# One queue for the first loads, queries ahead of the modulation's rows, and spare products in TensorE's pauses

## The reference, cut to what matters

```python
mod = (silu(L0_c) @ L0_wmod).reshape(4, 6, 1, -1)
sa, ca, ga, sb, cb, gb = (mod[:, i] for i in range(6))     # gates: sign(g) * max(|g|, 0.25)
h = layernorm(x) * (1 + ca) + sa
x = x + ga * dilated_attention(h, Wk, Wq, Wv, W_out, b_out)  # 4 heads, dilations 1, 2, 4, 8
h = layernorm(x) * (1 + cb) + sb
x = x + gb * (mx_quantised(h) @ mx_quantised(weight).T + bias)
mod = (silu(L1_c) @ L1_wmod).reshape(4, 6, 1, -1)            # the second layer's six
h = layernorm(x) * (1 + ca) + sa
x = x + ga * mamba(h, ...)      # conv of 4 taps, silu, a scan of 16 states over time, gate with silu(z)
h = layernorm(x) * (1 + cb) + sb
x = x + gb * gated_recurrence(h, ...)
```

## Time and profile before

| what | value |
|---|---|
| median of 3 runs | 1284.66 us (1284.48 to 1288.39) |
| the profiled execution | 1291.45 us, span 1290.1 us |
| TensorE busy | 1144.3 us, 89% of the span |
| VectorE busy | 1172.5 us, 91% |
| GpSimdE busy | 981.8 us, 76% |
| ScalarE busy | 781.7 us, 61% |
| mean granted TensorE clock | 0.968 |
| chain that ended last, by engine | PE 40%, DVE 28%, POOL 12%, issue 9%, ACT 6%, DMA 4% |
| first instruction of the first scan | 107.52 us from the span's start |

### The profile page before, as it was taken

The page is one execution under the profiler, slowest core; times in us unless marked ns, Lnnn a source line. Parts: engine busy times, 40 slices in busy tenths (PEclk is TensorE's granted clock), DMA queues, the critical chain, the costliest instruction groups (busy, mean ns, idle before and its releaser), DMA issues.

```text
span 1290.1 us, 12503 instructions
## 1 busy us (share of the span) xinstructions
PE 1144.3 (89%) x3574; PEld 640.0 (50%) x3574; DVE 1172.5 (91%) x1161; ACT 781.7 (61%) x1447; POOL 981.8 (76%) x713
## 2 busy tenths in 40 slices
PE   6767967898899989998999899998999898789896
PEld 4533523474447543673447543673447443444454
DVE  3666899999999999999999999999999999999987
ACT  2226645856667657855767657865776666645532
POOL 3213795889879897989878997989878996976852
PEclk9778988999999999999999999999999999899999
DMA  6406567775768678876769687876868676899922
GB/s 252 139 5 220 209 226 258 282 261 213 250 227 303 235 251 290 288 259 224 251 227 308 213 281 277 299 251 212 265 219 302 219 270 219 303 322 345 371 88 98
DMA packets 92309, 313.87 MB, mean 243 GB/s; under 512 B 10432, under 2 KB 15680, under 8 KB 91984
## 3 DMA queue, kind: packets, MB, share of 16 engines
q1 hardware_dynamic: 89216, 303.77, 68.1%
q10 hardware_dynamic: 3024, 9.31, 2.0%
HBM read 301.73 MB, written 11.31 MB: 243 GB/s over the span
## 4 chain that ended last, share of the span: by engine, by line
PE 40%; DVE 28%; POOL 12%; issue 9%; ACT 6%; DMA 4%; DVEq 0%; SPq 0%; POOLq 0%; ACTq 0%
DVE ps L1667 15%; PE ps L857 14%; POOL arena L1894 6%; PE ps L568 5%; DVE ps L1390 4%; PE ps L791 4%; DVE arena L1673 3%; PE ps L576 3%; DMA arena<-bc_scratch 2%; PE ps L695 2%; PE ps L703 2%; PE ps L711 2%; PE ps L718 2%; PE ps L600 1%; DVE stats_before L1271 1%
## 5 line engine op out<-in xcount | busy, mean ns | idle before, releaser
L1894 POOL TENSOR_TENSOR arena<-arena 128x1024 f32<-128x1024 f32 x255 | 600.2, 2361 | 157.3 <-PE ps L857 126.1
L1667 DVE TENSOR_TENSOR_SCAN ps<-ps,arena 128x1024 f32<-128x1024 f32 (+1 forms) x257 | 585.8, 2280 | 24.6 <-ACT ps L1236 15.8
L857 PE MATMUL ps<-arena,identF 128*128 128x512 f32 x1024 | 485.4, 605 | 47.2 <-DVE arena L1673 28.3
L1236 ACT ACTIVATE ps<-arena,negA 128x512 f32<-128x512 f32 x512 | 333.0, 683 | 87.4 <-DVE arena L1673 82.5
L857 PEld LDWEIGHTS ps<-arena,identF 128*128 128x128 f32 x1024 | 190.9, 194 | 267.6 <-issue 203.0
L1673 DVE TENSOR_TENSOR arena<-ps,arena 128x1024 f32<-128x1024 f32 x256 | 311.8, 1218 | 5.7
L872 ACT ACTIVATE arena<-arena,rnln 128x256 f32<-128x256 f32 x120 | 63.0, 589 | 50.9 <-POOL rnln L1700 37.6
L614 PE MATMUL ps<-arena,inw 128*128 128x512 f32 x128 | 62.5, 635 | 20.0 <-ACT arena L881 9.6
L1390 DVE SCALAR_TENSOR_TENSOR ps<-arena,vecs,ps 128x512 f32<-128x512 f32 x96 | 64.8, 747 | 5.9 <-ACT ps L985 5.9
L695 PE MATMUL ps<-arena,inw 128*128 128x512 f32 x128 | 61.1, 600 | 3.3 <-DVE arena L1554 3.3
L881 ACT ACTIVATE arena<-ps,modT 128x512 f32<-128x512 f32 x45 | 54.1, 1267 | 13.9 <-PE ps L454 13.5
(11 more groups left out here) (220 smaller groups left out, 1675.9 us busy)
## 6 DMA issues: line engine op xcount, KB each, us to landing
arena<-bc_scratch SPq DMA_DIRECT2D x511, 512.0 KB, 5.0
arena<-in_x SPq DMA_DIRECT2D x16, 256.0 KB, 6.7
arena<-in_x SPq DMA_DIRECT2D x8, 512.0 KB, 8.1
xr_scratch<-arena SPq DMA_DIRECT2D x6, 512.0 KB, 6.6
px_scratch<-arena SPq DMA_DIRECT2D x6, 512.0 KB, 7.0
out_x<-arena SPq DMA_DIRECT2D x5, 512.0 KB, 2.6
arena<-bc_scratch SPq DMA_DIRECT2D x9, 256.0 KB, 3.6
rowmod<-mod_scratch SPq DMA_DIRECT2D x4, 512.0 KB, 8.7
```

What stands on the lines that cost most here:

```text
L857: x = pe.matmul(ps[:, Y, :], identF[:], inp[:, m % RING, q, :], start=False, stop=(i == BLOCK_STEPS - 1 and q == 1), skip_group_check=True)
L1236: x = act.activation(ps[:, 2 * (m % 2) + q, :], dt[:, kd, :], ACT.Exp, scale=negA[:, kd, 2 * i + q:2 * i + q + 1])
L1667: x = dve.tensor_tensor_scan(states, states, inp[:, m % RING, q, :].rearrange("p q t -> p (q t)"), 0.0, ALU.mult, ALU.add)
L1894: x = pool.tensor_tensor(inp[:, m % RING, :, :], u[:, kd:kd + 1, :].broadcast_to([P, 2, TH]), b_at[:, m % 3, :, :], ALU.mult)
```

## The change

Three things are done, all in the part before the first scan.

The loads that ScalarE issued move to SP's queue, in a new order: after x (the wait on `xin`) come the small vectors, the query weights, the 1 MB of the modulation, the key weights, the value weights, the FFN weight, the output weights and the bias rows, and then what SP had behind them. The semaphore `qk_in` is split into `wq_in` and `wk_in`, and the FFN weight gets `wn_in`, so that the readers of the small vectors wait for two transfers and not three.

On TensorE the first query product moves ahead of the first two rows of the modulation. On VectorE the maximum of the first scores moves behind the second gate row.

`pe_idle(n)` issues n products of 128x128 by 128x512 into bank 3 that nothing reads: four behind the product that opens the sums, four behind the FFN, and one behind the transposes of the third layer norm.

```diff
@@ sp_first
             sp.wait_ge(S.xin, 32)
-            sp.dma_start(wm[:, 0, :, 2 * E:6 * E], d["wmod"][:, 0, :, 2 * E:6 * E]).then_inc(S.wmod0_in, 16)
             sp.dma_start(vecs[:, 0:40], d["vecs"]).then_inc(S.small_in, 16)
             sp.dma_start(negA[:], d["A_log"]).then_inc(S.small_in, 16)
-            sp.dma_start(wn.rearrange("p (j e) -> p j e", e=E), d["ffn_w"]).then_inc(S.small_in, 16)
+            sp.dma_start(wqT[:], d["wqT"]).then_inc(S.wq_in, 16)
+            sp.dma_start(wm[:, 0, :, 2 * E:6 * E], d["wmod"][:, 0, :, 2 * E:6 * E]).then_inc(S.wmod0_in, 16)
+            sp.dma_start(wkT[:], d["wkT"]).then_inc(S.wk_in, 16)
...
@@ pe_first
+        def pe_idle(n):
+            for _ in range(n):
+                pe.matmul(ps[:, 3, :], identF[:], wqT[:, 0:2, :, :].rearrange("p h k v -> p (h k v)"), start=True, stop=True,
+                          skip_group_check=True)
...
+            pe.wait_ge(S.wq_in, 16)
+            pe.wait_ge(ln["ln1"].out, 2)
+            pe_heads(wqT, 0, X0, S.q_mm)
             pe.wait_ge(S.wmod0_in, 16)
             pe_modulation_rows(0, 1)
-            pe.wait_ge(S.qk_in, 32)
-            pe.wait_ge(ln["ln1"].out, 2)
-            pe_heads(wqT, 0, X0, S.q_mm)
+            pe.wait_ge(S.wk_in, 16)
             pe_heads(wkT, 0, X1, S.k_mm)
...
@@ act_first
-            act.wait_ge(S.xin, 32)
-            act.dma_start(wqT[:], d["wqT"]).then_inc(S.qk_in, 16)
...
@@ dve_first
-            dve_smax(0, 1, 0)
             dve.wait_ge(S.modrow, 2)
             dve.tensor_scalar(modr[:, CB0, :], modr[:, CB0, :], 1.0, None, ALU.add).then_inc(S.modrow_step, 1)
             dve_gate_row(GB0, 5)
+            dve_smax(0, 1, 0)
             dve_rsum(0, 1)
-            dve.wait_ge(S.small_in, 48)
+            dve.wait_ge(S.wn_in, 16)
```

More of the change, by code:

```diff
@@ L109 @@
 LAST_ORDER, LAST_TANH = (0, 2, 4, 1, 3, 5), {1: X0, 2: 2}
-LOADS = ["cin_in", "wmodc_in", "wmod0_in", "wo_in", "ffn_in", "cpw_in", "wmod1_in", "small_in", "qk_in", "attn_in", "ssm_in",
+LOADS = ["cin_in", "wmodc_in", "wmod0_in", "wo_in", "ffn_in", "cpw_in", "wmod1_in", "small_in", "wn_in", "wq_in", "wk_in", "attn_in", "ssm_in",
          "rest_in", "xin", "xrow_in", "rowmod_in", "gate1_in", "dtx_in"]
@@ L334, in sp_first @@
             sp.wait_ge(S.xin, 32)
-            sp.dma_start(wm[:, 0, :, 2 * E:6 * E], d["wmod"][:, 0, :, 2 * E:6 * E]).then_inc(S.wmod0_in, 16)
             sp.dma_start(vecs[:, 0:40], d["vecs"]).then_inc(S.small_in, 16)
             sp.dma_start(negA[:], d["A_log"]).then_inc(S.small_in, 16)
-            sp.dma_start(wn.rearrange("p (j e) -> p j e", e=E), d["ffn_w"]).then_inc(S.small_in, 16)
+            sp.dma_start(wqT[:], d["wqT"]).then_inc(S.wq_in, 16)
+            sp.dma_start(wm[:, 0, :, 2 * E:6 * E], d["wmod"][:, 0, :, 2 * E:6 * E]).then_inc(S.wmod0_in, 16)
+            sp.dma_start(wkT[:], d["wkT"]).then_inc(S.wk_in, 16)
+            sp.dma_start(wvT[:], d["wvT"]).then_inc(S.attn_in, 16)
+            sp.dma_start(wn.rearrange("p (j e) -> p j e", e=E), d["ffn_w"]).then_inc(S.wn_in, 16)
+            sp.dma_start(woT[:], d["woT"]).then_inc(S.attn_in, 16)
+            sp.dma_start(bias_rows[:], d["bias_rows"].rearrange("(o a) e -> o a e", o=1).broadcast_to([P, 3, E])).then_inc(S.attn_in, 16)
             sp.dma_start(xrows[0], half_rows(0)).then_inc(S.xrow_in, 16)
@@ L527, in pe_first @@
                       skip_group_check=True).then_inc(S.sums_open, 1)
+            pe_idle(4)
             yield CHANNELS
@@ L540, in pe_first @@
             pe_transposes(hn3, 1, X1, ln["ln3"].mm)
+            pe_idle(1)
             yield CONVOLVE
@@ L887, in act_first @@
             act.activation(cTin[:], cTin[:], ACT.Silu).then_inc(S.silu_c, 1)
-            act.wait_ge(S.xin, 32)
-            act.dma_start(wqT[:], d["wqT"]).then_inc(S.qk_in, 16)
-            act.dma_start(wkT[:], d["wkT"]).then_inc(S.qk_in, 16)
-            act.dma_start(wvT[:], d["wvT"]).then_inc(S.attn_in, 16)
-            act.dma_start(woT[:], d["woT"]).then_inc(S.attn_in, 16)
-            act.dma_start(bias_rows[:], d["bias_rows"].rearrange("(o a) e -> o a e", o=1).broadcast_to([P, 3, E])).then_inc(S.attn_in, 16)
             act.wait_ge(ln["ln1"].nb, 1)
@@ L900, in act_first @@
             act_ln_cols("ln1", hB1, X0, 0, 0, 0, True)
-            act.wait_ge(S.small_in, 48)
+            act.wait_ge(S.small_in, 32)
             act.activation(negA[:], negA[:], ACT.Exp).then_inc(S.negA, 1)
@@ L1740, in pool_first @@
                 pool_mask(step)
-            pool.wait_ge(S.small_in, 48)
+            pool.wait_ge(S.small_in, 32)
             pool.tensor_scalar(vecs[:, VEC["D"]:VEC["D"] + 8], vecs[:, VEC["D"]:VEC["D"] + 8], 0.5, None, ALU.mult).then_inc(S.halved, 1)
```

## The result

| what | before | after |
|---|---|---|
| median of 10 runs each | 1288.22 us (1282.82 to 1292.15) | 1293.65 us (1292.23 to 1295.54) |
| ratio, 95% interval | | 1.0047 (1.003 to 1.0064) |
| the profiled execution | 1291.45 us, span 1290.1 us | 1293.53 us, span 1292.2 us |
| mean granted TensorE clock | 0.968 | 0.970 |
| first instruction of the first scan | 107.52 us | 109.75 us |

The account below looks back on a forecast made before the run. A chain through every engine bounds the kernel, with almost no slack in the first 82 us set-up. Savings of 0.7 + 0.5 + 1.9 = 3.1 us from the median 1284.66 gave 1281.6 us, range 1277.5 to 1285.5.

Parts of the forecast that it names:

- The gate row ahead of the first maximum: VectorE's gate row moved into its wait for scores: gating of woT starts 4.1 us earlier, worth nothing and costing nothing.
- Start: Loads and first queries: queries start at 14.23, 0.94 us earlier, no load waits; worth 0.7 us, about 2.4 at most.
- rival (d): The single queue delivers a load late, costing what exceeds the slack; 27% together with the clock lost in both pauses.
- First pause: Four spare products before the FFN's transposes: transposes gain 0.93 us, FFN loses the clock, its rise unmoved; worth 0.5 us.
- Second pause: Spare products between FFN and convolution: clock stays, convolution starts at full pace, VectorE's taps move with it; 1.9 us saved.
- its sign of being wrong: Saved time reappearing as a longer wait between convolution and first scan, or clock states varying by chance more than the gain.
- Rival (c): Spare products run at half pace and outlast their pauses: slower by 4.1 us, 1288.8 us; chance 6%.
- Rival (a): The clock holds from the first spare block through the FFN: 5.9 us saved, 1278.8 us; chance 22%.
- The Trainium skill's rule on transposes: Transposes do not count as busy for the clock as products do; by it alone the FFN would not keep the clock.

## Why the prediction was wrong

**The step that failed** is "The gate row ahead of the first maximum", which ended: "So this is worth nothing now, and costs nothing". It asked only who waits for GpSimdE's gating, and nobody does. It did not ask what the gating would run beside at its new time. The work moved from 37.98 to 31.54 us, onto VectorE's quantisation, which had lain alone between 31.82 and 36.7 us, and the instruction behind it on VectorE is the maximum that TensorE waits for. The price is 4.5 us, by the timelines set beside each other above, and 4.9 us by the kernel with that edit alone (0.38% of 1287 us; the interval is 2.8 to 7.0).

The trace of before had the evidence. Its two equal copies into `cT`, at 39.08 and 40.80 us beside GpSimdE's gating, took 1.79 and 1.21 us; in the changed kernel, with GpSimdE past its gating, they took 0.68 and 0.69, of which the first:

```profile
41.32 0.68 DVE L1440 COPY cT<-vecs 128x1024 f32<-128x1024 f32 x1
```

Two equal instructions of different length, with the other engine busy beside them, were the sign to price. GpSimdE's three operations take 6.2 us from start to end before (37.98 to 44.21), and the three operations of the quantisation that came to lie beside them are 1.8 us of work: held to the end, they would be some 4.4 us late. This is an estimate made afterwards.

The Trainium skill (SBUF — State Buffer, Who interferes with whom) says that VectorE and GpSimdE share a pair of ports that is held for a whole instruction, and that a VectorE operation with two inputs in SBUF, or a copy or tensor_scalar in a mode that uses both ports, stands still while a GpSimdE instruction that reads SBUF holds them. The traces agree, 2.46 against 0.43 us and 2.72 against 0.69; in which mode the one with a single input ran, no run shows. By that rule the step would have read some +4.4 us instead of 0, and the sum 1286.0 us with the start and both pauses as I had them.

The other steps, in their order:

- Start, "0.7 us". The queries started at 13.97 us (14.23 forecast), no load was late, and rival (d) did not happen. In the profile of the changed kernel TensorE was 2.24 us ahead before the hold, near the upper end of 2.4. Alone, the queue and the order gave 0.94 us at the first scan in the profiled execution, but move no median (ratio 1.0006, 0.9989 to 1.0024). Whether the term of 0.7 us was right stays open: it lies inside that interval.
- First pause, "0.5 us". The stage went nearly as forecast: 2.07 us idle (2.1), transposes in 1.49 us, between the 1.04 and 1.97 named, and the clock lost. They took 0.48 us less than before, but the FFN took 6.21 us and not 5.82 and gave 0.39 back; that its rise "does not move" was the weak step. In the kernels without the hold the idle rest is 5.4 us and not 2.1, because the 2.1 came from a pause measured at half pace.
- Second pause, "1.9 us". Right in its stage, 7.10 us against 8.98. Wrong behind it: the prediction ended the stretch that the change touches at the convolution, and its sign of being wrong named a longer wait there, not slower work. The idle 3.32 us behind the convolution stayed as long, but the work behind it lost its clock and cost 1.45 us (a lag of 0.77 us became 2.22), and alone the spare products change nothing (1.0001, 0.9984 to 1.0018). With three products in that gap the ratio is 0.998 (0.9963 to 0.9998), against 0.9998 without them; the two intervals overlap.
- Rival (c), the only one on the slow side, had another mechanism. No spare block in the traces read here ran at half pace (eight records took 3.60 us in the changed kernel), and the 9 products left out changed nothing. It got the sign of the result for no reason of its own, and was given 6%.
- Rival (a), the clock held through the FFN, is what eight products do: the FFN takes 3.69 us. With four it took 5.48 to 6.21 us in every trace.
- The Trainium skill's rule on transposes (TensorE: Matmul & The Clock Gate, Part 4, PE-mode transpose), which the prediction weighed, fits the changed kernel, where the clock fell during them, but doesn't decide alone: with the pause filled, 1.09 us of transposes and 0.83 us of waiting stand between the spare block and the FFN (60.71 to 62.63 us), and the FFN kept full pace.

**The base.** Three runs gave 1284.66 us; ten gave 1288.22. The prediction said that the profiled execution was 6.8 us slower than that median and took the lower number for the sum. Of the 12 us between its forecast and the result, 3.6 are this, 4.5 the hold, 3.1 the three gains that did not arrive at the end, and the rest, 0.9, lies within what such medians vary. That the gains did not arrive is best seen in the changed kernel with the old order on VectorE, which has all three and no hold: ratio 0.9998, and at the most 2.3 us by its interval. A part of them may be there.

## What to carry to other kernels

When a step is moved to an earlier time, ask not only who waits for it but what it will now run beside: a GpSimdE operation laid over VectorE operations with two inputs in SBUF, or over a float32 tensor_scalar or copy like those here, holds them until it ends, here 4.5 us in all for GpSimdE's three. Spare products are safest if they reach to the next work: rests of 2.07 and 5.4 us ahead of the transposes lost the clock, rests of 0.31 and 1.25 us kept it, and where the line lies isn't known. The pause has to be measured at the pace that they bring; it is then longer than the one in the old trace. A gain in one stage counts when the next pause has been looked at too.

## What the runs showed of the hardware

- The hold takes both kinds: a one-input TENSOR_SCALAR of 128x512 (0.43 us alone; int32 or float32) and a TENSOR_TENSOR with both inputs in `arena` (0.69 us alone) each ended 0.3 to 0.55 us after the GpSimdE operation beside them. A scan step with one input in PSUM is not held. In the kernel before it takes 2.30 us wholly beside GpSimdE, and 2.29 us where GpSimdE is idle:

```profile
111.33 4.91 POOL L1894 TENSOR_TENSOR arena<-arena 128x1024 f32<-128x1024 f32 x2 [0.94 <-DMA arena<-bc_scratch]
124.72 2.38 POOL L1894 TENSOR_TENSOR arena<-arena 128x1024 f32<-128x1024 f32 x1 [8.48 <-PE ps L857]
...
111.84 2.30 DVE L1667 TENSOR_TENSOR_SCAN ps<-ps,arena 128x1024 f32<-128x1024 f32 x1
...
121.50 2.29 DVE L1667 TENSOR_TENSOR_SCAN ps<-ps,arena 128x1024 f32<-128x1024 f32 x1
```

- It goes the other way as well: GpSimdE's product of 2.35 us took 2.60 us in the changed kernel and 2.73 us in the variant with the gate row alone, where VectorE was at work when it started, on an operation that ended 0.4 and 0.5 us later.
- The same idle 3.32 us behind the convolution kept the clock in five of nine traces and lost it in four. Kept, with 1.88 us for the projections: the kernel before, no spare products, the gate row alone, and queue and order alone, where the convolution took 8.71 to 9.14 us, and eight products in the first pause, where it took 7.11. Lost: the changed kernel, the gating held back, the old order on VectorE and spare products alone (3.01, 3.50, 3.57 and 3.55 us, the convolution at 7.1). Why it falls one way or the other isn't settled here.
